# Adding one to the normalised input: how a two-layer adaLN kernel gets its key sums, its state mask and its first bias rows

## What is computed

```
mod = (silu(c) @ wmod)                      # sa, ca, ga, sb, cb, gb per sample
h = layernorm(x) * (1 + ca) + sa
K = elu(h @ Wk + bk) + 1 ; Q = elu(h @ Wq + bq) + 1 ; V = h @ Wv + bv     # 16 heads of 8
KV = sum over tokens of K (x) V, per head ;  Ksum = sum over tokens of K
out = (Q KV) / (Q Ksum + 1e-6)
y = layer_norm(h + out @ Wo + bo)           # gains g1, beta1
x = x + ga * layer_norm(y + relu(y @ W1 + b1) @ W2 + b2)
h = layernorm(x) * (1 + cb) + sb
x = x + gb * sigmoid(xr @ W_r) * (relu(xk @ W_k)**2 @ W_v)   # xr, xk: token shift
```

## Time and profile before

| | before |
|---|---|
| median of 3 runs | 173.37 us (173.33 to 173.41) |
| the profiled execution, its own time | 173.09 us |
| its span | 171.4 us |
| TensorE matmuls busy | 160.8 us (94%) |
| TensorE weight loads busy | 148.7 us (87%) |
| VectorE | 137.3 us (80%) |
| ScalarE | 107.3 us (63%) |
| GpSimd | 106.8 us (62%) |

### The profile page before, as it was taken

How to read it: one execution, slowest core, us unless ns; L and a number is a source line. 1 busy time by engine, 2 the same in 40 slices (tenths; PEclk the granted TensorE clock), 3 DMA queues, 4 the chain that set the end, 5 groups by cost and what they waited for, 6 DMA issues and landing times. The chain is left out here.

```text
span 171.4 us, 4095 instructions
## 1 busy us (share of the span) xinstructions
PE 160.8 (94%) x1181; PEld 148.7 (87%) x1181; DVE 137.3 (80%) x618; ACT 107.3 (63%) x294; POOL 106.8 (62%) x235
## 2 busy tenths in 40 slices
PE   7995899999999999999989999999999999998883
PEld 7784689889999999999979999999999999787672
DVE  3644885989797979889896979797989788777852
ACT  3152573839393949586774949493939495737552
POOL 5233435575677777767695868676777756683531
PEclk9999999999999999999999999999999999999999
DMA  4529929900010101000010101010101010010012
GB/s 134 193 57 345 306 69 299 399 11 4 2 34 0 31 0 33 4 12 22 0 33 0 33 4 33 0 34 0 33 0 34 0 32 4 2 31 25 6 34 61
DMA packets 8347, 10.08 MB, mean 59 GB/s; under 512 B 723, under 2 KB 6534, under 8 KB 8326
## 3 DMA queue, kind: packets, MB, share of 16 engines
q1 hardware_dynamic: 7856, 9.54, 17.6%
q10 hardware_dynamic: 438, 0.28, 0.6%
q0 software_dynamic: 32, 0.01, 0.0%
HBM read 7.69 MB, written 2.13 MB: 57 GB/s over the span
## 5 line engine op out<-in xcount | busy, mean ns | idle before, releaser
L943 PE MATMUL bank<-w,hid 128*128 128x128 f32 x240 | 31.4, 275 | 0.0
L284 ACT ACTIVATE hT<-bank,modT 128x256 f32<-128x256 f32 x16 | 9.0, 565 | 35.4 <-PE bank L932 35.4
L975 PE MATMUL bank<-x1T,w 128*128 128x256 f32 x120 | 30.9, 380 | 0.0
L943 PEld LDWEIGHTS bank<-w,hid 128*128 128x128 f32 x240 | 29.0, 192 | 0.0
L975 PEld LDWEIGHTS bank<-x1T,w 128*128 128x128 f32 x120 | 21.5, 190 | 2.5 <-ACT x1T L288 0.2
L432 POOL TENSOR_TENSOR rstd_n<-vare_n,power 128x2 f32<-128x2 f32 x30 | 21.3, 708 | 2.4
L430 POOL TENSOR_TENSOR vare_n<-mv_n,eps 128x2 f32<-128x2 f32 x30 | 6.0, 200 | 18.9 <-DVE mv_n L540 18.9
L546 DVE TENSOR_SCALAR ny<-bank,mv_ny,rstd_ny 128x128 f32<-128x128 f32 x32 | 11.7, 406 | 5.4 <-POOL rstd_ny L432 5.4
L276 ACT ACTIVATE keepT<-bank,modT 128x255 f32<-128x255 f32 x28 | 14.3, 563 | 0.6 <-PE bank L932 0.6
L531 DVE BATCH_NORM_STATS2 stats_z<-bank 128x6 f32<-128x128 f32 x30 | 7.4, 289 | 8.2 <-PE bank L943 8.1
L430 POOL TENSOR_TENSOR vare_z<-mv_z,eps 128x2 f32<-128x2 f32 x14 | 2.8, 197 | 17.9 <-DVE mv_z L540 17.9
(11 more groups left out here) (176 smaller groups left out, 480.1 us busy)
## 6 DMA issues: line engine op xcount, KB each, us to landing
gm_rows<-mod_rows_dram SPq DMA_DIRECT2D x2, 960.0 KB, 9.0
out<-out_sb SPq DMA_DIRECT2D x15, 128.0 KB, 1.8
gm_rows<-mod_rows_dram SPq DMA_DIRECT2D x1, 768.0 KB, 6.2
w<-in_w SPq DMA_DIRECT2D x1, 512.0 KB, 4.9
bv_row<-bv_rows_dram SPq DMA_DIRECT2D x1, 512.0 KB, 11.7
x_all<-in_x SPq DMA_DIRECT2D x1, 384.0 KB, 4.4
bv_row<-bv_rows_dram SPq DMA_DIRECT2D x1, 384.0 KB, 5.5
gm_rows<-mod_rows_dram SPq DMA_DIRECT2D x1, 384.0 KB, 4.7
```

Of the source, the lines that this page charges most:

```text
L943: last = nc.tensor.matmul(banks[6][:, c * D:(c + 1) * D], hid[:, f, c * 128:(c + 1) * 128], w2[:, f, :], start=False, stop=(f == FF - 1 an ...
L975: return nc.tensor.matmul(bank[:, f % 2 * L:(f % 2 + 1) * L], w1[:, f * 128:(f + 1) * 128], x1T[:, :], start=True, stop=True)
```

## The change

Every n1 tile now holds n1 + 1. The features of n1 sum to zero for a token, so a product of (n1+1)^T K with a row weighted 1/128 gives Ksum times that row, and 16 columns of 1/128 give Ksum itself.

- ScalarE writes n1 + 1 (`take_n1`, at the end of its step t for sample t+1) with two Identity activations, scale rstd and bias 1 - mean*rstd. GpSimd makes this bias with two more small instructions (`first_scale`). VectorE's `next_n1` is gone.
- k_pair, its product with ones, kv_raw, the two masks on GpSimd and the Ksum column of a_sb are gone. The state product has a stationary a_sb of 128 columns and the moving tile wv_plus of 144: (1+ca) Wv plus the bias row, and 16 columns of 1/128. VectorE masks its result in one instruction from PSUM into kvs.
- wv_plus of sample t+1 is made in step t: ScalarE scales Wv (now behind a_sb), GpSimd adds the row (`plus_row`, behind ny's norm). The bias row is now `(sa - 1 - ca) @ Wv + bv`. For samples 0 and 1 (`DIRECT` = 2) TensorE makes the row on all partitions (`direct_rows`, 4 products of 128 columns) and VectorE adds it (`direct_weights`).
- The rows of the other samples: bv comes in as a one-row DMA on ScalarE's queue, TensorE adds it (`bv_product`, after K and Q of step 0), ScalarE copies the 16 rows out, and two loads bring them back. W1 and W2 are issued ahead of this.
- Three new columns for hT's bias and for the row are made on VectorE at the start. Two of the 16 keep_warm products are gone.

```diff
-BV_PARTS = ((0, 2), (2, 8), (8, 16))
+DIRECT = 2
+BV_PARTS = ((2, 8), (8, 16))
@@ SP
+            sp.dma_start(w12[:, :, :], a["w12"]).then_inc(w12_loaded, 16)
             sp.wait_ge(bv_ok, 1)
...
             load_bv(0)
-            sp.dma_start(w12[:, :, :], a["w12"]).then_inc(w12_loaded, 16)
+            sp.dma_start(x_all[:, 4 * NC:, :], x_dram[:, 4 * NC:, :]).then_inc(x_in[2], 16)
             load_bv(1)
-            sp.dma_start(x_all[:, 4 * NC:, :], x_dram[:, 4 * NC:, :]).then_inc(x_in[2], 16)
-            load_bv(2)
@@ ScalarE
+            act.wait_ge(pad_ok, 1)
+            act.dma_start(bv_pad[0:1, :], a["bv"].rearrange("(a d) -> a d", a=1)).then_inc(bv_loaded, 16)
...
+            def take_n1(s):
+                need(act, aks_mm, s - 1)
+                need(act, shift_n1_ok, s + 1)
...
+                for c in range(NC):
+                    last = nc.scalar.activation(n1[s % 2][:, c, :], x_all[:, NC * s + c, :], ACT.Identity,
+                                                scale=rstd["n1"][:, c:c + 1], bias=shift_n1[:, c:c + 1])
+                last.then_inc(n1_ok, 1)
...
                 if live(t):
-                    act.wait_ge(wvo_loaded, 16)
-                    need(act, kv_mm, sa)
-                    nc.scalar.activation(wv_mod[:, :], wv, ACT.Copy, scale=mod_col(CA, sa)).then_inc(wvm_ok, 1)
-                    need(act, aks_mm, sa + 1)
-                    nc.scalar.activation(a_sb[:, :], banks[3][:, 0:D + 1], ACT.Copy).then_inc(a_ok, 1)
+                    if t == 0:
+                        act.wait_ge(bv_mm, 1)
+                        nc.scalar.activation(bv_rows[:, :], banks[6][0:S, 2 * D:3 * D], ACT.Copy).then_inc(bv_ok, 1)
+                    need(act, aks_mm, sa + 1)
+                    nc.scalar.activation(a_sb[:, :], banks[3][:, 0:D], ACT.Copy).then_inc(a_ok, 1)
+                if DIRECT <= t + 1 < S:
...
+                    nc.scalar.activation(wv_mod[(t + 1) % 2][:, :], wv, ACT.Copy, scale=mod_col(CA, sa + 1)).then_inc(wvm_ok, 1)
...
+                if live(t + 1):
+                    take_n1(t + 1)
@@ GpSimd
+            def first_scale(s):
+                norm_scale("n1", s + 1)
+                need(pool, rstd_ok["n1"], s + 1)
+                nc.gpsimd.tensor_tensor(mean_r[:, :], mv["n1"][:, :, 0], rstd["n1"][:, :], ALU.mult).then_inc(mean_ok, 1)
+                need(pool, mean_ok, s + 1)
+                need(pool, n1_ok, s)
+                nc.gpsimd.tensor_tensor(shift_n1[:, :], one_pair[:, :], mean_r[:, :], ALU.subtract).then_inc(shift_n1_ok, 1)
+
+            def plus_row(s):
+                need(pool, wvm_ok, s - 1)
+                need(pool, kv_mm, s - 1)
...
+                pool.wait_ge(bv_in[part_of(BV_PARTS, s)], 16)
+                nc.gpsimd.tensor_tensor(wv_plus[s % 2][:, 0:D], wv_mod[s % 2][:, :], bv_row[:, s, :], ALU.add).then_inc(wvp_ok, 1)
...
-                if live(t):
-                    need(pool, aks_mm, sa)
-                    need(pool, k_ok, sa + 1)
-                    nc.gpsimd.tensor_tensor(k_pair[:, :], k_sb[:, 0, :], k_sb[:, 1, :], ALU.add).then_inc(pair_ok, 1)
...
+                if DIRECT <= t + 1 < S:
+                    plus_row(t + 1)
@@ VectorE
+            def direct_weights(s):
+                dve.wait_ge(direct_mm, DIRECT)
+                dve.wait_ge(wvo_loaded, 16)
+                nc.vector.scalar_tensor_tensor(wv_plus[s][:, 0:D], wv, modT[:, CA, s:s + 1], banks[2][:, s * D:(s + 1) * D],
+                                               ALU.mult, ALU.add).then_inc(direct_ok, 1)
...
                     need(dve, kv_mm, sa + 1)
-                    nc.vector.scalar_tensor_tensor(kv_raw[:, :], bv_row[:, sa, :], ksum, banks[3][:, 0:D],
-                                                   ALU.mult, ALU.add).then_inc(kvr_ok, 1)
+                    need(dve, u_mm, sa)
+                    nc.vector.tensor_tensor(kvs[:, :], banks[3][:, 0:D + H], mask[:, :], ALU.mult).then_inc(kvs_ok, 1)
@@ TensorE
+            def direct_rows():
+                pe.wait_ge(cols_ok, 3)
+                pe.wait_ge(wvo_loaded, 16)
+                pe.wait_ge(bv_loaded, 16)
+                for s in range(DIRECT):
+                    dest = banks[2][:, s * D:(s + 1) * D]
+                    nc.tensor.matmul(dest, modT[:, ROW, s:s + 1].broadcast_to([128, 128]), wv, start=True, stop=False)
+                    nc.tensor.matmul(dest, part128[:, :], bv_pad[:, :], start=False, stop=True).then_inc(direct_mm, 1)
...
-                if live(t):
-                    need(pe, pair_ok, sa + 1)
-                    nc.tensor.matmul(banks[3][:, D:D + 1], k_pair[:, :], ones[:, :], start=True, stop=True).then_inc(aks_mm, 1)
...
-                    need(pe, wvm_ok, sa + 1)
-                    nc.tensor.matmul(banks[3][:, 0:D], a_sb[:, 0:D], wv_mod[:, :], start=True, stop=True).then_inc(kv_mm, 1)
+                    if t < DIRECT:
+                        pe.wait_ge(direct_ok, t + 1)
+                    else:
+                        need(pe, wvp_ok, sa - 1)
+                    nc.tensor.matmul(banks[3][:, 0:D + H], a_sb[:, :], wv_plus[t % 2][:, :], start=True, stop=True).then_inc(kv_mm, 1)
```

More of the change, by code:

```diff
@@ L53, in build @@
         ident = sb("ident", [128, 128])
-        ones = sb("ones", [128, 1])
-        headmask = sb("headmask", [128, H, DH])
+        part128, bv_pad = sb("part128", [128, 128]), sb("bv_pad", [128, D])
+        mask = sb("mask", [128, D + H])
         power = sb("power", [128, NC])
@@ L92, in build @@
         qT = sb("qT", [128, L])
[L93 to L96, removed]
+        a_sb = sb("a_sb", [128, D])
+        wv_mod = [sb(f"wv_mod{p}", [128, D]) for p in range(2)]
+        wv_plus = [sb(f"wv_plus{p}", [128, D + H]) for p in range(2)]
+        mean_r, shift_n1, one_pair = (sb(n, [128, NC]) for n in ("mean_r", "shift_n1", "one_pair"))
         kvs = sb("kvs", [128, D + H])
@@ L431, in norm_scale @@
                 need(pool, vare_ok[name], count)
+                if name == "n1":
+                    need(pool, n1_ok, count - 1)
                 nc.gpsimd.tensor_tensor(rstd[name][:, :], vare[name][:, :], power[:, :], ALU.pow).then_inc(rstd_ok[name], 1)
-            norm_scale("n1", 1)
+            def first_scale(s):
[8 more added lines that the diff above has]
+                need(pool, kv_mm, s - 1)
+                if s == DIRECT:
+                    pool.wait_ge(const_pool, 9)
+                pool.wait_ge(bv_in[part_of(BV_PARTS, s)], 16)
+                nc.gpsimd.tensor_tensor(wv_plus[s % 2][:, 0:D], wv_mod[s % 2][:, :], bv_row[:, s, :], ALU.add).then_inc(wvp_ok, 1)
+            first_scale(0)
             def gate_weights(s):
@@ L714, in step @@
                 if live(t + 1):
+                    need(dve, mean_ok, sa + 1)
                     norm_mv("n1")
@@ L752, in step @@
                     q_elu()
-                if live(t + 1) and not (t == 1):
-                    next_n1()
+                if t == 0:
+                    direct_weights(0)
+                    direct_weights(1)
                 if live(t - 1) and not y_first:
@@ L1002, in step @@
                 if live(t - 1):
-                    need(pe, s16_ok, sb_ + 1)
-                    need(pe, kv_ok, sb_ + 1)
+                    need(pe, kvs_ok, sb_ + 1)
                     need(pe, q_ok, sb_ + 1)
@@ L1032, in step @@
                     if draining(t):
-                        need(pe, kvr_ok, S)
+                        need(pe, kvs_ok, S)
                         need(pe, hidb_ok, sd)
@@ L1046, in step @@
                     need(pe, k_ok, sa + 1)
-                    need(pe, kvr_ok, sa)
+                    need(pe, kvs_ok, sa)
                     for c in range(NC):
-                        nc.tensor.matmul(banks[3][:, 0:D], n1[t % 2][:, c, :], k_sb[:, c, :], start=(c == 0),
-                                         stop=(c == NC - 1))
+                        last = nc.tensor.matmul(banks[3][:, 0:D], n1[t % 2][:, c, :], k_sb[:, c, :], start=(c == 0),
+                                                stop=(c == NC - 1))
+                    last.then_inc(aks_mm, 1)
+                    if t == 0:
+                        keep_warm(2)
                 if live(t - 1):
```

93 lines of the change are left out of this document (44 added, 49 removed).

## The result

The changed kernel takes **168.47 us** as a median of 4 runs (167.6 to 169.76), the kernel before beside it 173.35 (172.96 to 173.41, 4 runs): a ratio of 0.9708, 95% interval 0.9653 to 0.9764. Forecast were 168.5, a range of 167.6 to 170.2, and "faster" with 0.94. The profiled execution took 168.26 us with a span of 166.3, against 173.09 and 171.4 before; 168.2 was forecast for it.

What follows compares the result with a forecast made beforehand. TensorE's own instruction list was taken to bound the full steps, waits the start and tail. Gains of 1.3 + 0.2 + 2.4 + 1.0 = 4.9 us gave 168.2 us profiled, 168.5 as a median, range 167.6 to 170.2.

Steps and rivals of the forecast that it cites:

- The start, 1.3: First u, no longer behind the bias row's DRAM round trip, comes at 13.6 instead of 14.87: 1.3 us gained.
- Steps 1 to 3, 0.2: Steps 1 and 2 stay set by ny; K's 0.20 us wait for hT goes: 0.2 us gained.
- Full steps, 2.4: Removing the pair product, less the wider state product, saves 0.20 us in each of 12 full steps: 2.4 us.
- Step 9, 1.0: The wait for k_pair behind GpSimd's tail weights goes, a wait of about 0.1 stays: 1.0 us gained.
- The next thing late is ny: In step 9, ny would be ready at 91.1 and TensorE want it at 90.9 to 91.0, about 0.1 us wait.
- The tail, nothing: The tail after the last steps keeps its work and order, so no gain.
- ScalarE's gate, 0.04: Rival, chance 0.04: n1 on ScalarE behind tanh_r exceeds its 0.58 us slack and gates the steps, slower, 175.0 us.
- The loads, nothing: Bias rows of samples 2 to 7, asked for at about 12.0, land by 23.7, before TensorE's need near 25: no cost.

Runs made afterwards that it cites:

- Experiment 10: The changed kernel unaltered, run six more times beside its variant with early tail mixing weights: 168.83 us, ratio 0.9728.
- Experiment 1: The kernel before, with zeros as bias rows of samples 0 and 1, so no wait for their DRAM round trip: 171.19 us, ratio 0.9903.
- Experiment 6: The changed kernel with GpSimd making the tail's mixing weights at the end of step 0, not in step 9: 169.44 us, ratio 0.9719.
- experiment 9: The changed kernel with three more 128x128 pieces on ScalarE ahead of n1 in steps 4 to 14: 170.05 us, ratio 0.9806.
- experiment 7: The changed kernel with n1 + 1 written by VectorE instead of ScalarE: 168.63 us, ratio 0.9688.
- 8: The changed kernel with one more 128x128 piece on ScalarE ahead of n1 in steps 4 to 14: 168.89 us, ratio 0.9714.
- 11: The changed kernel with the tail's mixing weights made at the end of step 0, run again six times: 169.38 us, ratio 0.974.
- experiment 2: The kernel before without the product of k_pair and ones from sample 1 on, TensorE still waiting for k_pair: 172.15 us, ratio 0.986.
- 3: The kernel before without the product of k_pair and ones from sample 1 on and without TensorE's wait for k_pair: 170.03 us, ratio 0.9819.
- 4 to 11: All on the changed kernel; the first two add one product in steps 4 to 15, of one column (170.66 us) and of 128 columns (170.32).

## Why the prediction was right, point by point

- **The start, 1.3.** Experiment 10 and the kernel before have the same pace and the same K (8.28 and 8.29), so their first u compare cleanly: 13.38 against 14.87, 1.49 gained. What was named as late next, n1 of sample 1 behind a_sb on ScalarE, is what is late: the transposition loads at 11.87 with a wait of 0.36 for it. It was put at 11.95 there and u at 13.6; TensorE needed 1.51 from there to u and not 1.64. The term that was mis-sized is that distance: I took 0.30 for its last warm product, the length of its load, where u's load stands 0.23 behind it (13.15 to 13.38 in experiment 10); and what follows the transposition stands 0.17 behind it (11.87 to 12.04), not 0.22. Experiment 1 has the wait removed and nothing added, and reaches u at 12.89, but its pace rose earlier; counted from K, u comes 4.87 behind in experiment 1 and 5.10 in experiment 10. So the detour over ScalarE and the products for the rows cost 0.2 of what removing the wait alone gives.
- **Steps 1 to 3, 0.2.** From the first to the fourth u 0.23 more. TensorE's waits for ny stay in steps 1 and 2, 1.38 and 0.27, as forecast. The one of 0.41 in step 3 was not in the forecast: there too ny now sets the next u, which comes 8.09 behind the one before and not 8.25.
- **Full steps, 2.4.** 0.20 in each of 11 periods, and shown from both sides: taking the product out of the kernel before gives 0.22 to 0.23, putting one column into the changed kernel costs 0.18, 128 columns 0.22.
- **Step 9, 1.0.** This is where the forecast failed in a step. The wait for k_pair did go, but the period came down by 0.94, with the product's 0.20 in it: 0.74 instead of 1.0. "The next thing late is ny" was wrong. ny was ready by 88.51, 0.06 ahead of its load. The next thing late was mixT, behind x pieces that took 1.20 in place of 0.61; the longer x had stood in the timeline of before as well, covered by the wait. Experiment 6 shows the cause by taking GpSimd's mixing instructions away from there: 8.77. Yet ny was late as well. It is over 8.65 behind u, exactly as in the kernel before and not at the 8.5 of my sum, and TensorE, had it lost nothing at mixT, would have come for it 8.33 behind u as in step 8. By the timeline a mixT in time would thus have left a wait of about 0.3 at ny, not 0.1. No run here tries that.
- **The tail, nothing.** It gave 0.26. At the last u the gain is 4.84, and where ny of the last sample is transposed it is 5.08. Before, that load stood at 153.62 with a wait of 0.30 for ny; now it stands at 148.54, with no wait marked. VectorE's chain ahead of it (from prod over mv_z to attT's input) runs 0.17 shorter. Why was not tried.
- **ScalarE's gate, 0.04.** The slack is 0.95 in the timeline, about 1.0 by experiment 9, and not 0.58. The 0.37 come from two things: tanh_r starts 6.02 behind u and not 6.24, since it moves with the products ahead of it, which my sum had left in place; and n1 starts at 77.38, ahead of tanh_r's end at 77.48, where I had put it behind the end with 0.04 more.
- **The loads, nothing.** The rows of samples 2 to 7 are asked for at 11.7 and land 3.5 later. GpSimd adds the first of them at 19.2 without a wait.

The sum by these: 1.48 + 0.23 + 2.2 + 0.94 + 0.26 = 5.1 of span, against 4.9; the executions' own times differ by 4.8. The step 9 that I overrated, and the start and the tail that I underrated, nearly cancel. And 168.47 is a median of four runs of which one belongs to the slower group; six later runs gave 168.83.

## What to carry to other kernels

In a full TensorE list an f32 product of up to 128 columns costs its two passes, nearly whatever its columns (0.18 for one, 0.22 for 128): remove it whole, or fold it as extra columns into a product that is there anyway (16 more columns cost 0.02). When a long wait is removed, look in the timeline of before for instructions under its cover that are slower than in the neighbouring steps; those are what is late next. And compare starts only between profiles whose TensorE came up to its pace at the same moment.

## What the runs showed of the hardware that I had not expected

- **The moment at which TensorE comes up to its pace differs from run to run.** With the same warm-up from 1.12 on, two loads went from 0.55 to 0.30 between about 4.5 (experiment 7) and about 10.6 (experiment 6), and of the profiles of the changed kernel and its variants those with a late rise were in the slower group of their runs (experiments 6, 8 and 11), those with an early one in the faster. The granted clock of the stretches says 1.00 at the slow pace too, so only the durations tell. That the activity releases a slower default, at a moment that the kernel does not set, is what the Trainium skill says (TensorE: Matmul & The Clock Gate, section What's actually happening); these traces agree. It puts the spread between runs at half a microsecond either way; here it is 6 us in all, and the measurement decides.
- **A wait at the start can cost the pace a second time.** In experiment 2 TensorE waited 1.78 us for the first u behind the round trip, and then its granted clock fell. In the profile of the kernel before it waited 1.62, and the clock stayed at 1.00. Timeline and stretches of experiment 2:

```profile
14.44 0.54 PEld L1008 LDWEIGHTS bank<-kvs,qT 128*128 128x128 f32 x4 [1.78 <-issue]
15.12 0.98 PEld L1018 LDWEIGHTS bank<-kqvo,hT 128*128 128x128 f32 x4
...
15.00:16.00 1.00, 1.00 (x7) 0.91 (x6) 0.56 (x4) 0.00 (x0) 0.14 (x1) 0.50 1.06 327
18.00:19.00 1.00, 1.00 (x7) 0.83 (x7) 0.95 (x5) 0.92 (x4) 0.00 (x1) 0.82 1.06 291
```

  The clock is at its lower level, 1.2 GHz, from about 15 to 18, and the next u comes 7.91 later instead of 6.86. Of the 37 runs of kernels with this wait (29 of the kernel before, beside the experiments, and 8 of experiments 2 and 3) 18 had a mean granted clock below 0.995; of the 47 runs of kernels without it (the changed one, and experiments 1 and 4 to 11) none had. Experiment 1, which takes out the wait alone, is 7 of these 47. So it seems that the removed round trip also removes this risk; that each of the 18 lost its clock at this place is not shown, since experiment 2's profile is the only one of them here. Experiment 2's median of 172.15 is higher than its periods alone would make it.
- **VectorE's x pieces, of 128 columns from two tiles in SBUF, take twice as long (0.61 to 1.20) beside GpSimd's instructions of 256 columns.** Shown is that the delay goes when GpSimd's work is moved (0.61 in experiments 6 and 11); how the two engines get in each other's way no run here shows.
